# An attention layer and a gated second layer: how the reciprocals of the softmax sums reach the rows of their heads

## The reference

```python
q, k, v = heads(LN(LN(x)) @ Wq), rope(heads(LN(ctx) @ Wk)), heads(LN(ctx) @ Wv)   # 16 heads of 64
attn = softmax(clip(q @ k.T / 8, -11, 11))
x = x + (attn @ v).reshape(B, 256, 1024) @ Wo + bo
# second layer on LN(x): attention among 16 groups of 8 features per token,
# an output product, then sum over 8 experts of gate[e] * (h2 @ We[e])
```

## Time and profile before

| | us |
|---|---|
| median of 3 runs | 390.94 (389.09 to 391.6) |
| the profiled execution | 388.52 |
| its span, first to last instruction | 386.4 |
| TensorE busy in it | 321.9 (83%) |
| VectorE busy | 269.6 (70%) |
| GpSimd busy | 217.0 (56%) |
| ScalarE busy | 155.5 (40%) |

### The profile page before, as it was taken

The page is one execution under the profiler, slowest core; times in us unless marked ns, Lnnn a source line. Parts: engine busy times, 40 slices in busy tenths (PEclk is TensorE's granted clock), DMA queues, the critical chain, the costliest instruction groups (busy, mean ns, idle before and its releaser), DMA issues.

```text
span 386.4 us, 6595 instructions
## 1 busy us (share of the span) xinstructions
PE 321.9 (83%) x2566; PEld 215.9 (56%) x2566; DVE 269.6 (70%) x459; ACT 155.5 (40%) x282; POOL 217.0 (56%) x200
## 2 busy tenths in 40 slices
PE   6699999999999989789999999599998986630444
PEld 6476666667776656457766566377665545310131
DVE  4886426337754799777585999774549879599844
ACT  3464544555324546215345556343444540100500
POOL 4767344355544483929346677973445876546070
PEclk9999999999999999969999999999999999755656
DMA  8730000000000000000000000000000000000000
GB/s 248 181 53 2 27 2 1 2 2 3 0 2 2 1 2 0 3 0 2 2 0 2 1 2 2 1 15 2 1 2 0 2 3 14 0 0 0 0 0 27
DMA packets 10157, 5.82 MB, mean 15 GB/s; under 512 B 2768, under 2 KB 9744, under 8 KB 10128
## 3 DMA queue, kind: packets, MB, share of 16 engines
q1 hardware_dynamic: 9072, 5.29, 5.3%
q10 hardware_dynamic: 1056, 0.13, 0.2%
HBM read 4.89 MB, written 0.52 MB: 14 GB/s over the span
## 4 chain that ended last, share of the span: by engine, by line
PE 53%; DVE 23%; POOL 10%; issue 6%; ACT 5%; DMA 2%; SPq 1%; DVEq 0%; POOLq 0%; ACTq 0%
PE sc L493 11%; PE pv L507 11%; PE sums L523 5%; POOL prod L823 5%; PE pj_k L434 5%; DVE prod L815 4%; PE pj_k L436 4%; PE pj_k L435 4%; DVE att L1003 4%; ACT e L688 3%; DVE o L1020 3%; PE side L580 3%; DMA prod<-in_L_xattn_Wq_dram 2%; DVE prod L823 2%; POOL wvS L1212 1%
## 5 line engine op out<-in xcount | busy, mean ns | idle before, releaser
L688 ACT ACTIVATE e<-sc 128x1024 f32<-128x1024 f32 x64 | 65.7, 1026 | 100.9 <-PE sc L493 100.9
L1225 POOL TENSOR_SCALAR e<-e 128x1024 f32<-128x1024 f32 x64 | 71.6, 1119 | 34.7 <-ACT e L688 30.9
L1218 POOL TENSOR_TENSOR krot<-kcos,ksin 128x512 f32<-128x512 f32 x32 | 41.7, 1304 | 69.7 <-DVE ksin L903 69.7
L493 PE MATMUL sc<-qs,ks 64*128 64x256 f32 x768 | 62.5, 295 | 6.3 <-ACT e L688 5.7
L493 PEld LDWEIGHTS sc<-qs,ks 64*128 64x128 f32 x768 | 49.4, 185 | 28.5 <-issue 16.6
L507 PE MATMUL pv<-e,v 128*64 128x256 f32 x512 | 64.0, 393 | 0.0
L507 PEld LDWEIGHTS pv<-e,v 128*64 128x64 f32 x512 | 34.5, 139 | 24.2 <-issue 9.3
L903 DVE TENSOR_TENSOR kcos<-pj_k,cosT 128x512 f32<-128x512 f32 x32 | 22.0, 688 | 30.2 <-PE pj_k L436 29.8
L523 PE MATMUL sums<-e,sum_rows 128*32 128x256 f32 x512 | 30.9, 382 | 5.3 <-POOL e L1225 5.3
L840 DVE TENSOR_TENSOR ks<-krot,ks 128x512 fp32r<-128x512 f32 x32 | 34.0, 1063 | 0.0
L823 POOL TENSOR_TENSOR prod<-att,kv 128x1024 f32<-128x1024 f32 x8 | 27.7, 3474 | 8.9 <-ACT att L779 8.6
(11 more groups left out here) (215 smaller groups left out, 596.3 us busy)
## 6 DMA issues: line engine op xcount, KB each, us to landing
ctx_in<-in_ctx_dram SPq DMA_DIRECT2D x4, 256.0 KB, 5.0
prod<-in_L_xattn_Wkv_dram SPq DMA_DIRECT2D x2, 512.0 KB, 6.0
x_in<-in_x_dram SPq DMA_DIRECT2D x1, 512.0 KB, 5.8
prod<-in_L_xattn_Wq_dram SPq DMA_DIRECT2D x1, 512.0 KB, 6.6
wo<-in_L_xattn_Wo_dram SPq DMA_DIRECT2D x1, 512.0 KB, 8.4
fwe<-in_L_ffn_We_dram SPq DMA_DIRECT2D x1, 512.0 KB, 4.3
out_dram<-x_in SPq DMA_DIRECT2D x4, 128.0 KB, 1.8
fbup_r<-in_L_ffn_bup_dram SPq DMA_DIRECT2D x1, 128.0 KB, 6.5
```

The source lines that it names most:

```text
L493: last = nc.tensor.matmul(sc[:, h, c * NT:(c + 1) * NT], ks[rows, j % 3, k_part, chunk], qs[rows, j % 2, q_part, :], start=(k_part + q_par ...
L688: nc.scalar.activation(e[:, j % 3, :, 2 * half:2 * half + 2, :].rearrange("p h c n -> p h (c n)"), sc[:, :, :], ACT.Exp, scale=SCALE).then ...
L1218: nc.gpsimd.tensor_tensor(krot[:, j % 2, :], kcos[:, j % 2, :], ksin[:, j % 2, :], ALU.add)\
L1225: nc.gpsimd.tensor_scalar(a, a, EXP_HIGH, EXP_LOW, ALU.min, ALU.max).then_inc(s_clip, 1)
```

## The change

The reciprocals are no longer spread over the rows of their heads by matmuls. SyncE copies them: for each pair and each head one DMA reads the 8 rows of rec that hold the head's reciprocals, each 8 times (a source pattern [8, 8, 256] with a step of 0 in the middle), and writes the head's 64 rows of a new tile rec_rows, 64 KB. That is 16 DMAs per batch; four raise one semaphore each for norm_i. VectorE's multiply stands where it stood, waits for that semaphore and reads rec_rows instead of a bank. The high and low parts of rec, the matrix spread, its set-up on GpSimd (L1203 to L1207) and its cast on VectorE (L1137 to L1139) are gone, and so are the side steps norm0 to norm3 on TensorE. The multiplication is by rec in full float32. On SyncE the 64 DMAs of all four batches stand before the first output store.

```diff
+            for b in range(NB):
+                sp.wait_ge(s_rec, b + 1)
+                for p in range(PAIRS):
+                    if p % 2 == 0 and b:
+                        sp.wait_ge(s_norm, 4 * (b - 1) + p // 2 + 1)
+                    for h in range(2):
+                        row = 32 * (2 * (p % 2) + h) + 8 * (p // 2)
+                        sp.dma_start(rec_rows[DH * h:DH * h + DH, p, :], rec[row:row + 8, :].unsqueeze(1).to_broadcast([8, 8, NT]))\
+                            .then_inc(s_rec_rows[p // 2], 16)
             for b in range(NB):
                 if b < NB - 1:
                     sp.wait_ge(s_y, TT * (b + 1))
...
-                elif name.startswith("norm"):
-
-                    if name == "norm0":
-                        pe.wait_ge(s_recS, b + 1)
-                    if name == "norm0" and b == 0:
-                        pe.wait_ge(s_spread, 1)
-                    for i in range(2):
-                        p = 2 * int(name[4]) + i
-                        dst = side[:, i * NT:(i + 1) * NT]
-                        nc.tensor.matmul(dst, spread[:, p, :], recS[:, 0, :], start=True, stop=False)
-                        last = nc.tensor.matmul(dst, spread[:, p, :], recS[:, 1, :], start=False, stop=True)
...
                             if t == 0 and p % 2 == 0:
-                                pe.wait_ge(*taken(f"norm{p // 2}", b))
+                                pe.wait_ge(s_norm, 4 * b + p // 2 + 1)
...
                 nc.vector.reciprocal(rec[:, :], sum_bank[:, 0:NT]).then_inc(s_rec, 1)
-                dve.wait_ge(s_rec, b + 1)
-                own(nc.vector.tensor_copy(recS[:, 0, :], rec[:, :]))
-                split_lo(recS[:, 1, :], rec[:, :], recS[:, 0, :]).then_inc(s_recS, 1)
...
+            def normalise_outputs(i, b):
+                dve.wait_ge(s_u, PAIRS * b + 2 * i + 2)
+                if i == 0 and b:
+                    dve.wait_ge(*made("out_proj", b - 1))
+                if i == 0 and b >= 2:
+                    dve.wait_ge(s_y, TT * (b - 1))
+                dve.wait_ge(s_rec_rows[i], 64 * (b + 1))
+                nc.vector.tensor_tensor(flat(on[:, 2 * i:2 * i + 2, :]), flat(u[:, 2 * i:2 * i + 2, :]),
+                                        flat(rec_rows[:, 2 * i:2 * i + 2, :]), ALU.mult).then_inc(s_norm, 1)
...
-                if slot == 0:
-                    dve.wait_ge(s_const, 3)
-                    nc.vector.tensor_copy(spread[:, :, :], spread_f[:, :, :]).then_inc(s_spread, 1)
```

## The result

| | before | after |
|---|---|---|
| median of the compared runs, us | 391.27 | 399.66 (4 runs, 398.28 to 400.48) |
| ratio, 95% interval | | 1.0234 (1.0197 to 1.027) |
| profiled execution, us | 388.5 | 399.25 |
| its span, us | 386.4 | 397.3 |
| mean granted clock of TensorE | 0.930 | 0.913 |

The loss is clear of the noise. Whether it is more than 2% is left open by the interval.

What follows compares the result with a forecast made beforehand. TensorE was taken to bound the attention slots (53% of the chain), VectorE and GpSimd mostly the tail. Middle +2.5 and tail +10.8 gave +13.3 us on 390.9, so 404; range 388 to 417, the forecast's own 397 to 412.

Steps and rivals of the forecast that it cites:

- the tail: After batch 3's reciprocal: the reduction queued behind norm3 is 10.8 us late, with nothing to cover it; +10.8 us.
- P: Copies into rec_rows: the pace at which the DMAs follow one another, taken as 1.07 us, bounded by 0.48 and 1.28.
- L: Copies into rec_rows: time of one DMA to landing, taken as 1.8 us from the output store.
- T: Time from a batch's reciprocal until norm3's data is there: L + 15 x P, 17.9 us.
- rival B: Copies in between, P about 0.7: T = 12.3, middle -4.2, tail +5.3, 392 us; chance 0.15.
- rival A: Transfers hidden, SyncE's issue sets P at 0.48: middle -4.2, tail +2.0, sum -2.2, 389 us; chance 0.20.
- C: Rival: reading few places limits and all DMAs queue on it, P = 1.28; sum +25.8, 417 us; chance 0.20.
- port rule: Copies' source: 8 neighbouring partitions lie on two ports of about 27 GB/s, 64 KB takes 1.2 us, sum near 412.
- The middle: Batches 0 to 2: norm3's late data less 1.4 us saved each gives +1.3, -0.6 and +1.8; +2.5 us.
- The removal: Norm matmuls leaving TensorE in batches 0 to 2: 3 x 1.4 = 4.2 us saved at most.
- rival D: Real gain: all 16 matmuls of three batches count, copies at issue pace, clock stays up; -5.5, 385 us; chance 0.05.
- The multiply by two SBUF operands: VectorE's norm_i multiply reading rec_rows: taken as 0.7 us, with 0 to 0.4 us more each possible.

## Why the prediction was right in kind and 4 us too high

**The forecast, slower by the tail, held.** 404 was predicted, 399.7 measured: +8.4 where the sum gave +13.3. All of the loss lies where the prediction put 10.8 of the 13.3, in the reduction queued behind norm3 after the last reciprocal. The forecast's own range, 397 to 412, holds the result (its lower end, P = 0.95, works out to 398).

**L and P, the two halves of T, were both mis-sized.** I had L = 1.8 us from the output store and P = 1.07 from the repeated rows, with SyncE's 0.48 as the lower bound. The chain of waits of the changed kernel in the tail shows issues and a landing (start us, us):

```profile
317.04 0.62 SPq L428
...
317.71 0.61 SPq L428
...
319.02 0.98 SPq L428
...
320.98 1.21 SPq L428
...
328.94 4.46 DMA rec_rows<-rec
```

An issue takes 0.61 us and 0.04 follow it; some are stretched to 0.9 or 1.2. Over batch 0's twelve DMAs from norm0 to norm3 the pace is 0.77 us each, and 0.83 in batch 1 and in the tail. Behind the last issue come 4.46 us to landing (3.47 behind norm2's in batch 0), not 1.8. Worked back by the formula, L = 6.57 - 3 x 0.77 = 4.3. So rival B's pace came with a landing time that no rival had: T for norm0 was 6.6 instead of 5.0, and for norm3 15.9 to 16.5 instead of 17.9. SyncE's issue, which rival A rested on, is what the chain names, but at 0.61 and not 0.48, and stretched; whether the few places read are what stretches it is not shown. C's mechanism is real, but belongs to the form that reads one row over two places: there 1.21 us, near C's 1.28, and 434 us.

**The Trainium skill's port rule** was applied to one DMA alone: two ports, 1.2 us, sum near 412. The four DMAs of a norm_i are in flight together and by the rule lie on four ports. The estimate by it is then 0.61, below what was measured. That eight engines would just about attain the issue pace was said without a row for it; issues took 0.61 us and the pace was 0.77.

**The middle: +2.5 predicted, -2.3 in the trace (-0.5, -2.0, +0.2), -0.7 to -3.0 in the compared times.** T was the term that failed. With norm3's measured starts (15.9, 16.3, 16.0) as T against the same limits (15.2, 17.1, 14.7) and the same 1.4 us, the procedure gives -0.7, -1.4 and -0.1, sum -2.2. That this meets the trace's -2.3 is in part luck: single stretches scatter by 1 to 3 us, and in batches 1 and 2 norm3 started when VectorE was free (behind L1039) and not when its rows came, so 16.3 and 16.0 are upper bounds of T. And the procedure did not see who waits. I had the values' wait for the key products "inside norm3's delay". In batch 0 it is the wait (0.90 us), and norm3 comes just in time for out_proj.

**The removal: 4.2 predicted, 7.0 by the ratio.** Batch 0's 1.40 us is the term. Batch 1's 4.4 is more: there the clock did not fall ahead of the value product, as in rival D, which gave 5.8 + 1.7 = 7.5 for the middle. Which part of the 7.0 is the clock's is not shown; it was not varied alone. Most of it was lost again to late rows.

**The tail: +10.8 predicted, 11.55 in the trace up to the sum** (23.61 against 12.06). The reduction was 9.4 us late (17.08 behind the reciprocal's end instead of 7.71), 1.4 less than predicted by the smaller T. The 20 matmuls of out_proj left by then took 4.53 us and not 2.3, with the clock at 0.55 from 334 to 339, and this added 2.2. The prediction had named the clock's fall in the tail as a cost in its range, at 1.7, and not in its sum. That 10.8 comes so near 11.55 is luck: two errors of opposite sign.

**The multiply by two SBUF operands.** 0.69 us in most cases, as taken, but norm0 took 1.42 in batch 0, 1.26 in batch 1 and 1.53 in the tail. None of these delayed anything that the trace shows: the next multiply still waited for its own rows (0.81, 0.50 and 1.52 us), and norm3 took 0.68 or 0.69 each time.

**The lines that were named to show it.** Right: norm3 16 us behind the reciprocal, VectorE waiting for the DMA, the tail's reduction 17 us behind it. Wrong: out_proj did not start 14 us behind the reciprocal's end and stretch; it started 15.5 to 15.8 behind it in the three batches and took its usual 3.73.

## What to carry over

Moving work off the engine that bounds a steady loop is worth only what the replacement's latency leaves: here 7.0 us were there, and late rows took all but 1 to 3 of them. The same latency at the end of the program, where nothing overlaps it, is paid in full, so cost the last round separately, and keep the short path there. For a train of small DMAs, take the issue time of one and the time from the last issue to landing as two terms, and look at what else stands in queue order behind each multiply that will wait for it.

## What the runs showed of the hardware

- SBUF to SBUF, 64 KB with each source row read eight or 64 times: 3.5 to 4.9 us to landing while others are under way, 0.6 us to issue in the median, and 0.77 to 0.86 us apart. With one row read and the two heads' rows 32 apart: 1.21 us apart, 4.5 to 7.2 us to landing (median 5.8).
- Reading the second head's copy four partitions further on, from a row with the same values, was worth 33.5 us of 434. A DMA share of 0.75 instead of 0.41 brought no better pace (0.86 against 0.77 us).
- TensorE had waited 8.6 us in the tail when out_proj began at 0.50 of the clock; its 32 matmuls took 6.68 us so, and 3.74 us when useless matmuls had filled the wait.
- The clock's fall in the middle is not tied to one place: low at 165 to 171 us before (0.52), full there without the matmuls and copies (1.00), low at 248 to 258 in a kernel whose code for that batch was as before (0.73).
